# The transposed one-hot matrix of a graph kernel on VectorE by one compare instead of on ScalarE by two passes

## The reference, cut to what matters

```
s_src = jnp.sum(proj * gat_a_src, -1)
s_tgt = jnp.sum(proj * gat_a_tgt, -1)
e = jax.nn.leaky_relu(s_src[src] + s_tgt[tgt], 0.2)
exp_e = jnp.exp(e - jnp.max(e))
denom = jax.ops.segment_sum(exp_e, tgt, num_segments=n)
attn = exp_e / (denom[tgt] + 1e-16)
agg = jax.ops.segment_sum(proj[src] * attn[:, :, None], tgt, num_segments=n)
```

```
dA = jnp.exp(dt[:, :, None] * A)
dBx = (dt * xc)[:, :, None] * Bm[:, None, :]
def step(h, t):
    dA_t, dBx_t, C_t = t
    h = dA_t * h + dBx_t
    return (h, h @ C_t)
```

## Time and profile before

| | us |
|---|---|
| median of 3 runs (lowest, highest) | 4460.03 (4455.53, 4463.82) |
| the profiled execution, its own time | 4442.53 |
| its span, first to last instruction | 4440.7 |
| busy in the span: DVE | 3093.5 (70%) |
| PE | 2961.1 (67%) |
| POOL | 2309.8 (52%) |
| ACT | 2050.7 (46%) |

### The profile page before, as it was taken

One profiled execution on the slowest core, in us unless ns is written; L12 is line 12 of the kernel. 1 busy time (PEld: TensorE's weight loads), 2 busy tenths in 40 slices (PEclk: granted clock), 3 DMA queues, 4 the chain that ended last, 5 costly groups with the idle time before them and its releaser, 6 DMA issues. The chain is left out here.

```text
span 4440.7 us, 65579 instructions
## 1 busy us (share of the span) xinstructions
PE 2961.1 (67%) x16509; PEld 2169.8 (49%) x16510; DVE 3093.5 (70%) x5833; ACT 2050.7 (46%) x4280; POOL 2309.8 (52%) x2215
## 2 busy tenths in 40 slices
PE   5343220377777777777777777777776389948998
PEld 4333210254555545555455555554554245527887
DVE  5677793688888878788788788778887568831111
ACT  2000000366666666566666566665665356622222
POOL 2000004576666666666666676666666237643443
PEclk8555555699889888889888898988888699969999
DMA  3000201344444444444444444444446523226665
GB/s 105 24 0 0 96 1 59 102 124 121 118 121 121 118 121 118 114 123 121 121 121 116 116 124 118 122 114 118 124 119 107 115 55 100 84 87 152 143 143 110
DMA packets 282992, 457.08 MB, mean 103 GB/s; under 512 B 56487, under 2 KB 203160, under 8 KB 282392
## 3 DMA queue, kind: packets, MB, share of 16 engines
q0 software_dynamic: 119472, 287.74, 27.3%
q1 hardware_dynamic: 163176, 165.34, 13.0%
HBM read 389.45 MB, written 63.43 MB: 102 GB/s over the span
## 5 line engine op out<-in xcount | busy, mean ns | idle before, releaser
L677 POOL DMA_INDIRECT el_g<-table,el_ix x1792 | 1776.2, 991 | 863.8 <-issue 516.8
L1097 PE MATMUL fl_ps<-el_g,el_oh 128*128 128x260 f32 x3584 | 1074.7, 452 | 535.8 <-DVE ACC L792 525.0
L1097 PEld LDWEIGHTS fl_ps<-el_g,el_oh 128*128 128x128 f32 x3584 | 770.7, 224 | 945.7 <-issue 778.0
L812 DVE TENSOR_TENSOR_SCAN mb_h<-mb_dA,mb_h,mb_dB 128x224 f32<-128x224 f32 x896 | 575.0, 672 | 257.3 <-issue 206.4
L782 DVE TENSOR_TENSOR el_g<-el_g,fl_pw 128x1024 f32<-128x1024 f32 x448 | 542.6, 1211 | 0.0
L974 ACT ACTIVATE mb_dA<-mb_dt,mb_a 128x224 f32<-128x224 f32 x898 | 382.4, 475 | 145.7 <-DVE mb_dt L872 144.0
L1120 PE MATMUL fl_py<-mb_hc,ident 128*128 128x448 f32 x896 | 431.9, 564 | 0.0
L959 ACT CAST el_oh<-fl_pt 128x512 f32<-128x512 bf16 x451 | 260.2, 577 | 331.2 <-PE fl_pt L1073 330.4
L468 POOL DMA_INDIRECT sorted_x<-XN,rank x49 | 47.6, 972 | 589.1 <-DVEq L388 574.4
L945 ACT ACTIVATE el_away<-el_dst,el_less 128x512 bf16<-128x512 bf16 x452 | 325.2, 720 | 21.0 <-DVE mb_a L746 20.9
L1997 POOL DMA_INDIRECT out<-ex_y,ex_to x112 | 174.1, 1554 | 278.5 <-DVE ex_y L1956 253.9
(11 more groups left out here) (297 smaller groups left out, 5245.0 us busy)
## 6 DMA issues: line engine op xcount, KB each, us to landing
el_dst<-dst_rows SPq DMA_DIRECT2D x452, 128.0 KB
el_g<-table,el_ix POOLq DMA_INDIRECT x1792, 2.8
ex_w<-in_moe_W SPq DMA_DIRECT2D x56, 512.0 KB
ex_x<-routed_x SPq DMA_DIRECT2D x56, 257.0 KB, 2.7
mb_x<-sorted_x SPq DMA_DIRECT2D x30, 224.0 KB, 2.7
table<-px_tr POOLq DMA_DIRECT2D x49, 130.0 KB, 2.3
px_x<-in_x SPq DMA_DIRECT2D x49, 128.0 KB, 3.0
xn<-XN SPq DMA_DIRECT2D x1, 6272.0 KB
```

The lines of the kernel that those rows point to most:

```text
L677: pool.indirect_dma_start(out=G[b // GU][:, b % GU * NJ + j, :], out_offset=None, in_=dram["table"], in_offset=bass.IndirectOffsetOnAxis(a ...
L812: nc.vector.tensor_tensor_scan(H[:, n % 2, k, :], dA[:, n % 2, k, :], dB[:, n % 2, k, :], H0[:, k, n % NS:n % NS + 1], ALU.mult, ALU.add). ...
L1097: mm = nc.tensor.matmul(pS, OH[:, n % (2 * GU), j, :], G[n // GU % 2][:, n % GU * NJ + j, :], start=j == 0, stop=j == NJ - 1)
```

## The change

`one_hot` goes from ACT to DVE. It is one instruction instead of two: `tensor_scalar` with `is_equal` compares the bf16 row `DST` with the partition's number (an fp32 column) and writes `OHT` in bf16. `AWAY` and `LESS` (the negated partition number) go, with one small instruction that made LESS. On DVE the compare of S+4 stands at the end of slot S, behind the inflow of S+1 and ahead of the read_out of S. SP's load of a new row into a `DST` buffer waits on the compare of the row it replaces, where it waited on ACT's first pass.

```
@@ -707,7 +706,7 @@
-                    sp.wait_ge(s["away"], p.number - 3)
+                    sp.wait_ge(s["hot"], p.number - 3)
@@ -876,6 +874,17 @@
+            def one_hot(p):
+
+                q, n = p.number, p.n
+                dve.wait_ge(brought[n % 4], p.of(4) * 16 + 16)
+                if not early(q, 2):
+
+                    dve.wait_ge(s["turned"], q - 1)
+                    dve.wait_ge(s["spread"], q - 1)
+                nc.vector.tensor_scalar(OHT[:, n % 2, :], DST[:, n % 4, :], w["part"][:, 0:1], None, ALU.is_equal
+                                        ).then_inc(s["hot"], 1)
@@ -917,7 +926,10 @@
                 if not last:
                     prepare(c + 1, 1 - b, at)
                     inflow(S + 1)
-
+                    one_hot(S + GU)
+
+            for u in range(GU):
+                one_hot(Slot(0, u))
@@ -934,21 +946,7 @@
-            def one_hot(p):
-
-                q, n = p.number, p.n
-                act.wait_ge(brought[n % 4], p.of(4) * 16 + 16)
-                if not early(q, 1):
-                    act.wait_ge(s["hot"], q)
-                nc.scalar.activation(AWAY[:], DST[:, n % 4, :], ACT.Abs, bias=LESS[:, 0:1]).then_inc(s["away"], 1)
-                if not early(q, 2):
-
-                    act.wait_ge(s["turned"], q - 1)
-                    act.wait_ge(s["spread"], q - 1)
-                act.wait_ge(s["away"], q + 1)
-                nc.scalar.activation(OHT[:, n % 2, :], AWAY[:], ACT.Relu, bias=1.0, scale=-1.0).then_inc(s["hot"], 1)
@@ -1031,7 +1029,6 @@
-                one_hot(S + GU)
                 keep_turned(S + (GU - 1))
@@ -1047,10 +1044,8 @@
-            one_hot(Slot(0, 0))
-            for u in range(1, GU):
-                one_hot(Slot(0, u))
-                keep_turned(Slot(0, u - 1))
+            for u in range(GU - 1):
+                keep_turned(Slot(0, u))
```

More of the change, by code:

```diff
@@ L599, in both_loops @@
     s = {n: sem(f"fl_{n}") for n in (
-        "cleared", "index", "dst", "away", "hot", "turned", "turned_sb", "spread", "logit", "shifted", "weight", "scaled", "summed",
+        "cleared", "index", "dst", "hot", "turned", "turned_sb", "spread", "logit", "shifted", "weight", "scaled", "summed",
         "added", "top", "all", "passed",
@@ L614, in both_loops @@
         OH, OHT = sb("el_oh", [P, 2 * GU, NJ, P]), sb("el_oht", [P, 2, SC], BF16)
-        DST, AWAY = sb("el_dst", [P, 4, SC], BF16), sb("el_away", [P, SC], BF16)
-        LESS, I16, S8 = sb("el_less", [P, 1]), sb("el_ident", [P, P], BF16), sb("el_s8", [P, GU * NJ, 2 * NH])
+        DST, I16, S8 = sb("el_dst", [P, 4, SC], BF16), sb("el_ident", [P, P], BF16), sb("el_s8", [P, GU * NJ, 2 * NH])
         Z, L, DM, Q, EM = (sb(f"el_{n}", [P, GU * NJ, NH]) for n in ("z", "l", "dm", "q", "em"))
@@ L740, in _ @@
             nc.vector.memset(H0[:], 0.0).then_inc(s["set"], 1)
-            nc.vector.tensor_scalar(LESS[:], w["part"][:], -1.0, None, ALU.mult).then_inc(s["set"], 1)
             nc.vector.tensor_copy(I16[:], w["ident"][:]).then_inc(s["set"], 1)
@@ L747, in _ @@
             dve.wait_ge(s["cleared"], 2)
-            dve.wait_ge(s["set"], 8)
+            dve.wait_ge(s["set"], 7)
             def logits(p):
@@ L936, in _ @@
             nc.scalar.activation(AE[:], A[:], ACT.Exp).then_inc(s["rate"], 1)
-            act.wait_ge(s["set"], 8)
-            def one_hot(p):
-                q, n = p.number, p.n
-                act.wait_ge(brought[n % 4], p.of(4) * 16 + 16)
-                if not early(q, 1):
-                    act.wait_ge(s["hot"], q)
-                nc.scalar.activation(AWAY[:], DST[:, n % 4, :], ACT.Abs, bias=LESS[:, 0:1]).then_inc(s["away"], 1)
-                if not early(q, 2):
-                    act.wait_ge(s["turned"], q - 1)
-                    act.wait_ge(s["spread"], q - 1)
-                act.wait_ge(s["away"], q + 1)
-                nc.scalar.activation(OHT[:, n % 2, :], AWAY[:], ACT.Relu, bias=1.0, scale=-1.0).then_inc(s["hot"], 1)
+            act.wait_ge(s["set"], 7)
             def keep_turned(p):
@@ L1063, in _ @@
             pe.wait_ge(s["weights"], 144)
-            pe.wait_ge(s["set"], 8)
+            pe.wait_ge(s["set"], 7)
             def turn(p):
```

## The result

| | before, us | changed, us |
|---|---|---|
| median of 4 runs each (lowest, highest) | 4461.92 (4455.53, 4472.20) | 4535.75 (4535.37, 4543.17) |
| the profiled execution | 4442.53 | 4535.66 |
| busy: DVE | 3093.5 | 3221.4 |
| ACT | 2050.7 | 1501.6 |
| TensorE's mean granted clock | 0.827 | 0.812 |

All but 1 us of it lies in the stage with the slots, whose first inflow moves from 864.1 to 865.0 us and whose last from 3484.5 to 3578.8.

What follows compares the result with a forecast made beforehand. The slot stage was taken as a chain through DVE, the fullest engine, in dense slots and through PE and ACT at chunk steps. 61 + 10 - 8 - 3 = +60 us on 4460 gave 4520 us; own range 4487 to 4559, overall 4475 to 4602.

Steps and rivals of the forecast that it cites:

- The compare's price: Each added DVE compare: 353 ns, pushing followers by 0.27 to 0.28 us, with POOL's gathers 0.31 us.
- Which compares count: Those opening slots 1, 2, 5, 7, 8, 14 and 15: 196 compares at 0.31 us, +61 us.
- covered: Compares opening slots 0, 3, 4, 6, 9 to 13 cost nothing, since waits for PE or ACT hide them.
- The late matrix: PE's turn and spread wait for the compare: up to 0.18 us late in slots 8 and 15, +10 us.
- Slot 9 keeps its length: Slots 9, 12 and 0 were to keep their length, with shorter waits of DVE.
- the first rival: Every compare counts, as longer gaps put more PE work at the lower clock: +139, 4599 us; chance 0.13.
- The gather waits: Where logits wait for the gather (20 times, 30.9 us), a slower DVE only takes from that wait: -8 us.
- Ahead of the first slot: Four pairs of ACT passes before its first chunk steps go: -3 us (0 to -5).
- ACT's relief in the slots: ACT loses 610 us of work; none of the 448 in the slots is on the path, credited 0.
- POOL's queue: Rival: compares wait until POOL's gather issue in flight is over, 0.36 us more each: +131, 4591 us; chance 0.07.
- the plain slots: Slots where DVE has no gap: 3.69 us from inflow to inflow, to lengthen to 4.0 us.
- the rival "faster": ACT's passes are in the chain of five decays a chunk that DVE waits for: -59, 4401 us; chance 0.10.

Runs made afterwards that it cites:

- the late turn alone: Kernel before with PE's turn of S+3 also waiting for DVE's inflow of S, no DVE work added: 4904.49 us (1.0023), repeated 4891.20 us (1.0036).
- both sets: The first two sets of experiments, each on another chip, where the kernel before takes 4,894 and 4,874 us.
- the compare alone: Kernel before with the compare added on DVE into a spare tile nobody reads, ACT still making the matrix: 4912.31 us (1.0040), repeated 4896.59 us (1.0067).
- set 2: Second set of experiments, on a chip where the kernel before takes 4,874 us; the changed kernel there took 4904.61 us (1.0088).

## Why the prediction was right

4520 us were forecast and 4535.75 measured; the forecast's own range was 4487 to 4559 (its upper end should read 4551: 92 + 10 - 8 - 3 = 91 us above 4460). The direction and the main mechanism, the compare's own time in the slots where DVE is dense, came true. That the size came so near is in part luck, as the steps show:

- **The compare's price: right.** 353 ns from the line through the earlier trace rows, 351 measured; the mean in the stage is 376 ns (168.2 us for 448), so the neighbours on POOL add 0.025 us, 0.03 forecast. The push is 0.26 in most slots, 0.27 to 0.28 forecast, and 0.40 in the three slots named above.
- **Which compares count: right where nothing but DVE works.** Slots 1, 2, 5, 7, 14 and 15 were forecast at 6 x 0.31 plus 0.18 for slot 15's late turn, 2.04 us a chunk, and grew by 1.69. Slots 0, 6, 11, 12 and 13 kept their length within 0.17 us, as forecast. In slot 3 the compare counted and slot 4 gave it back (0.24 and -0.33), which comes to the same as "covered".
- **The late matrix: the term that was too small.** It was put at +10 us in all, 0.18 in slots 8 and 15. In slot 15 it isn't seen: with the late turn alone its median is 3.68 us in both sets, as in a plain slot before. Slot 8 grew by 0.97 instead of 0.31 + 0.18, 14 us more than its two terms. I priced the turn and the spread and overlooked the load of the tile's number between them, which a turn that waits no longer hides; the gap of 0.45 us stands in slot 8's timeline, and it appears without a compare as soon as the turn is late, and goes when the load is moved.
- **Slot 9 keeps its length: wrong in these traces.** Slots 9 and 10 grew by 19 us. I had read one chunk, with 3.52 us at a clock of 0.54, as all of them. 12 of 27 ran at full clock, and these became slow. It is what I had put into the first rival (longer gaps put more of PE's work at the lower clock), in one place and not by every compare counting. In the changed kernel PE stands still 2.15 us ahead of these sums in 25 of 27 chunks, and the clock falls 0.7 to 2.2 us before they start. In the kernel before it stands 1.54 to 1.65 us in 18 chunks, and 11 of those sums ran wholly at full clock; in the nine with 2.2 us or more one did. That the longer wait made the clock fall was not tested by itself; one group of sums in the changed kernel was slow behind a wait of 1.53 us. On the other chips 3 to 10 of 27 sums ran at full clock in every kernel traced with the old order of the output, changed or not: 3 in the changed kernel both times, 10 and 5 with the compare alone. The kernel before has no trace there, so whether this term cost anything on those chips isn't known.
- **The gather waits: -15 us of DVE's waits for the gather** (30.9 to 16.3), -8 forecast. How much time that gave is not separable: slot 4 lost 0.33 us a chunk, slot 0 nothing.
- **Ahead of the first slot: -3 forecast, +1 measured.** The gain came and was lost again: ACT's copy out of PE's first product (`mb_xr`) starts 1.9 us earlier, but the three groups of matmuls behind it (L1126, L1154 and L1161 in the kernel before) took 1.78, 0.93 and 1.02 us at a granted clock of 1.00 there, and 3.35, 1.70 and 1.86 at 0.50 in the changed kernel. So here too matmuls lost the full clock, though PE's wait ahead of the first of them is 0.68 us in both kernels (before, then changed):

```profile
848.61 1.78 PE L1126 MATMUL fl_pm<-mb_xt,mb_wi 128*128 128x224 f32 x8 [0.68 <-ACT mb_xr L985]
```

```profile
846.73 3.35 PE L1121 MATMUL fl_pm<-mb_xt,mb_wi 128*128 128x224 f32 x8 [0.68 <-ACT mb_xr L983]
```

- **ACT's relief in the slots, credited at nothing: open.** ACT's busy time fell by 549 us (610 forecast: that sums the passes' own records, which overlap their neighbours'), and its waits grew. But -16 us, clear of zero, were measured for the relief on a slower chip, with a fixed matrix, and there is no such run on the first.

POOL's queue did not keep the compare out: its longest is 586 ns, where that rival wanted waits of up to 0.9 us. Of the 448 compares in the slots 336 begin while a gather's issue is under way, DVE stood idle before none of them, and the 150 that begin in its first 0.4 us take at most 359 ns. By the Trainium skill ("SBUF — State Buffer", section "SBUF: two separate sides") a VectorE operation that uses both ports and a GpSimd operation lock each other out for the whole instruction; neither nor these compares agree.

Against the traces the sum was 33 us short, 60 against 93: the plain slots were put too high (57 us against 47), slots 8, 9 and 10 too low (14 against 46), and the -8 and -3 did not come as time, or only in part. The forecast of the median is nearer because the medians moved by 74 us where the profiled executions moved by 93; which of the terms is smaller in an ordinary execution of the kernel before, no trace shows. Two readings in the prediction were loose and carried nothing: in the kernel before the logits of slot 12 wait for PE in 27 of 28 chunks and those of slot 8 never do, and the rival "faster" needed 0.44 us a decay, not more than half a microsecond.

## What to carry to other kernels

An instruction moved to the fullest engine costs what it pushes (here 0.26 of its 0.35 us), counted only where no wait behind it would have swallowed it; the emptied engine earns little if it waits for others behind the work removed. Then look at what stands in the queue of the engine that now waits: a small load of a register behind the wait comes on top. And before a wait is called steady, read it in all its repetitions: one that has a short and a long form can lose the short one. The best find was not the change but the chain it made visible: 90 and 109 us by the medians (79 and 100 by the ratios) for an output issued ahead of sums that did not need to be first.

## What was not expected of the hardware

The chips differ by 9 to 10%. On the three that ran the experiments the instructions have the durations of the first (the compare's median is 346 to 349 ns against 351, the scans' mean 670 to 674 against 672 and 673), and the parts ahead of the slots are alike. But in the stage PE, ACT and DVE stand still some 60 to 75 times, for up to 8 us, while a matmul that ACT should follow is long past; ACT and DVE go on within 0.1 us of each other. One such place, in the changed kernel of set 2:

```profile
1548.32 0.39 PE L1068 MATMUL fl_pt<-el_ident,el_oht 128*128 128x128 bf16 x4
...
1549.60 1.92 PE L1092 MATMUL fl_ps<-el_g,el_oh 128*128 128x260 f32 x8
...
1551.88 0.95 POOL L676 DMA_INDIRECT el_g<-table,el_ix  x1 [0.30 <-issue]
1555.05 0.59 ACT L957 CAST el_oh<-fl_pt 128x512 f32<-128x512 bf16 x1 [9.53 <-remote]
1555.15 0.62 DVE L799 TENSOR_TENSOR mb_dB<-mb_u,fl_pbc 128x448 f32<-128x448 f32 x1 [5.98 <-remote]
```

DVE's inflow, which never waits on the first chip (1.0 us in 449), waits 208.3 us in 73 times here, for something the trace doesn't name. In this place POOL issues two gathers more while ACT and DVE stand, and what both of them wait for is work of PE. Its cause stays open. On the first chip the same wait takes 4.87 or 6.83 us, by TensorE's level in the sums before it; what decides that level is open too.
